# Last group of tiles exchanged and finished tile by tile, its stores halved over two queues; the weight preparation and the first loads rearranged

## The reference

```python
w = weights[conditions]                       # 64 rows of a table of 200, each 64 x 64
y = einsum('bct,bcd->bdt', x, w)              # x is 64 x 64 x 512 float32
a = quant_dequant_mxfp4(y.reshape(-1, 512))   # blocks of 32 along the last axis
w = quant_dequant_mxfp4(weight)               # 512 x 512
out = x + (einsum('mk,nk->mn', a, w) + bias).reshape(...)
```

## Time and profile before

| | |
|---|---|
| median of 3 runs | 98.33 us (97.95 to 99.38) |
| the profiled execution | 97.9 us |
| its span | 96.2 us (1.7 us lie around it) |
| busy: PE, DVE, ACT, POOL | 84.4, 81.9, 75.3, 32.9 us |
| chain that ended last, shares by engine | PE 44%, ACT 11%, DVE 10%, issue 6% |
| read from and written to HBM | 10.49 MB, 8.39 MB |

### The profile page before, as it was taken

One profiled execution on the slowest core, in us unless ns is written; L12 is line 12 of the kernel. 1 busy time (PEld: TensorE's weight loads), 2 busy tenths in 40 slices (PEclk: granted clock), 3 DMA queues, 4 the chain that ended last, 5 costly groups with the idle time before them and its releaser, 6 DMA issues.

```text
span 96.2 us, 2263 instructions
## 1 busy us (share of the span) xinstructions
PE 84.4 (88%) x715; PEld 41.2 (43%) x715; DVE 81.9 (85%) x138; ACT 75.3 (78%) x85; POOL 32.9 (34%) x60
## 2 busy tenths in 40 slices
PE   5999594999799998999899899989999989989800
PEld 4966252595482324344233433333352333445300
DVE  1248999999999999999999999999979999885600
ACT  4740498699998869999999999999999849957000
POOL 4273758399647548303000300320040021054000
PEclk9999999999999999999999999999999999999995
DMA  1898789694896789799999991896579399486992
GB/s 34 288 316 295 244 249 301 212 352 125 181 317 218 274 248 269 242 312 265 254 310 298 311 212 49 272 245 116 218 185 224 114 263 222 88 272 175 270 285 92
DMA packets 13901, 22.17 MB, mean 230 GB/s; under 512 B 4034, under 2 KB 4802, under 8 KB 13890
## 3 DMA queue, kind: packets, MB, share of 16 engines
q1 hardware_dynamic: 11456, 17.31, 56.4%
q0 software_dynamic: 2432, 4.73, 23.6%
q10 hardware_dynamic: 2, 0.00, 0.0%
HBM read 10.49 MB, written 8.39 MB: 196 GB/s over the span
## 4 chain that ended last, share of the span: by engine, by line
PE 44%; ACT 11%; DVE 10%; issue 6%; ACTq 0%; DVEq 0%
PE o_ps L357 20%; PE y_ps L357 5%; PE y_ps L306 5%; ACT y_sb L471 5%; ACT o_sb L493 4%; PE o_ps L352 4%; PE o_ps L337 3%; DVE a L654 3%; DVE n_int L625 2%; DVE top L645 2%; ACT z L463 1%; PE o_ps L382 1%; PE y_ps L367 1%; PE y_ps L300 1%; PE y_ps L318 1%
## 5 line engine op out<-in xcount | busy, mean ns | idle before, releaser
L357 PE MATMUL o_ps<-wT,aT 128*128 128x512 bf16 x100 | 23.8, 380 | 0.4 <-ACT aT L508 0.4
L183 POOL DMA_DIRECT2D mix<-in_L_cond_weights_dram x32 | 17.9, 560 | 12.4 <-issue 11.0
L625 DVE TENSOR_TENSOR n_int<-y_sb,inv 128x1024 int16<-128x1024 f32 (+1 forms) x17 | 19.5, 1155 | 0.2
L306 PE MATMUL y_ps<-x_sb,mix 64*64 64x512 f32 x120 | 15.6, 606 | 3.9 <-DMA mix<-in_L_cond_weights_dram 2.4
L272 POOL DMA_DIRECT2D x_sb<-o_sb x6 | 6.1, 1014 | 35.1 <-ACT o_sb L493 35.1
L382 PE MATMUL o_ps<-idle 128*128 128x128 bf16 x214 | 16.6, 235 | 1.2 <-DVE idle L664 1.2
L463 ACT ACTIVATE z<-y_ps 128x1024 bf16<-128x1024 bf16 x16 | 16.2, 1039 | 1.5 <-PE y_ps L306 1.2
L471 ACT COPY y_sb<-y_ps 128x1024 f32<-128x1024 f32 x16 | 16.3, 1035 | 0.0
L382 PEld LDWEIGHTS o_ps<-idle 128*128 128x128 bf16 x214 | 13.6, 105 | 5.1 <-issue 4.7
L480 ACT ACTIVATE zone<-inv 128x1024 int16<-128x1024 int16 (+2 forms) x11 | 11.6, 1074 | 3.8 <-DVE inv L618 3.8
L502 ACT COPY aT<-o_ps 128x1024 bf16<-128x1024 bf16 x14 | 13.7, 1045 | 1.0 <-PE o_ps L337 1.0
(11 more groups left out here) (52 smaller groups left out, 76.0 us busy)
## 6 DMA issues: line engine op xcount, KB each, us to landing
x_sb<-in_x_dram SPq DMA_DIRECT2D x7, 1024.0 KB, 6.4
out_dram<-x_sb SPq DMA_DIRECT2D x15, 256.0 KB, 3.6
x_sb<-o_sb POOLq DMA_DIRECT2D x6, 512.0 KB, 5.2
out_dram<-x_sb SPq DMA_DIRECT2D x6, 512.0 KB, 3.1
w_sb<-in_L_ffn_weight_dram SPq DMA_DIRECT2D x4, 256.0 KB, 3.4
x_sb<-in_x_dram SPq DMA_DIRECT2D x2, 512.0 KB, 6.6
out_dram<-x_sb POOLq DMA_DIRECT2D x4, 256.0 KB, 3.6
mix<-in_L_cond_weights_dram POOLq DMA_DIRECT2D x32, 16.0 KB, 4.5
```

The lines of the kernel that those rows point to most:

```text
L183: queue.dma_start(mix[HALVES[i % 2], first + i // 2, :], table[bass.ds(row, 1), :, :].rearrange("o c d -> (o c) d")).then_inc(mix_in[step] ...
L306: last = nc.tensor.matmul(y_ps[HALVES[g], 2 * q + r, :], mix[HALVES[r], (step - 1) * GROUP + n, :], x_tiles(step, n)[HALVES[r], :], start= ...
L357: last = nc.tensor.matmul(o_bank(step, t), aT[:, t, c, :], wT[:, c, :], start=False, stop=(c == KC - 1))
L625: nc.vector.tensor_tensor(columns(n_int, t, n), columns(y_sb[:, step % 2, :, :], t, n), columns(inv, t, n), ALU.mult).then_inc(n_done, 1)
```

## The change

The last step's second pair is exchanged like all others, so its residual and stores need x in exchanged order: a new tile `last_x` (1 MB) holds step 8's x once more, loaded by four DMAs behind all other loads on SP. DVE adds into it tile by tile, and each tile is stored in two DMAs of 64 partitions, one by SP and one by ACT; the last tile as two column halves, each again by both. In step 8 every stage is done tile by tile (before: first two together).

Step 7 is done in pairs: `limit` and `rescale` by pairs, transposes of a pair follow them, the products by pairs. Its first pair has the residual through PE and POOL stores it, as before. Of the second, tile 2 goes to `o_sb` and through an accumulating DMA (256 KB) and tile 3 is added by DVE and stored by SP. The store of step 6's second pair moves from SP to POOL.

At the start, `top_zone`, `invert`, `limit` and `zone` of W are done by pairs, the transposes of W's first pair move ahead of the second mixing, and the two loads of step 1's x move from SP to ACT, behind ACT's work on W's first two tiles. SP issues the mixing matrices of step 2 ahead of x of step 2. The range assertions are left out of `load_mixes`.

```diff
+        last_x = sb("last_x", [P, GROUP, T], F32)
...
             _, rows = nc.values_load_multi_w_load_instructions(
-                cond_sb[:, 2 * first:2 * (first + len(tiles))], engines=[engine], min_val=0, max_val=S - 1)
+                cond_sb[:, 2 * first:2 * (first + len(tiles))], engines=[engine], min_val=0, max_val=S - 1,
+                skip_runtime_bounds_check_because="cond holds row numbers of the table")
...
+        def store_last(queue, t, g, part, done):
+
+            queue.dma_start(exchanged_dram[LAST - 1, t // 2, g, t % 2, :, part], last_x[HALVES[g], t, part]
+                            ).then_inc(done, 16)
...
-            for h in range(2):
-                sp.dma_start(x_tiles(1, 2 * h, 2).rearrange("p (n t) -> p n t", n=2),
-                             x_dram[:, 2 * h:2 * h + 2, :]).then_inc(x_first_in[h], 16)
             sp.wait_ge(cond_in, 16)
             load_mixes(sp, mybir.EngineType.SP, sp_mix_in, 1, SP_TILES)
+            load_mixes(sp, mybir.EngineType.SP, sp_mix_in, 2, SP_TILES)
             load_x(2)
-            load_mixes(sp, mybir.EngineType.SP, sp_mix_in, 2, SP_TILES)
...
+            for q in range(2):
+                for g in range(2):
+                    sp.dma_start(last_x[HALVES[g], 2 * q:2 * q + 2, :],
+                                 exchanged_x_dram[LAST - 1, q, g, :, :, :].rearrange("r c t -> c r t")
+                                 ).then_inc(last_x_in, 16)
...
-                sp.wait_ge(x_added[step % 2], 16 * ((step + 1) // 2))
-                store(step, SUMMED, GROUP - SUMMED)
+                if step < LAST - 2:
+                    sp.wait_ge(x_added[step % 2], 16 * ((step + 1) // 2))
+                    store(step, SUMMED, GROUP - SUMMED)
+            sp.wait_ge(added, 1)
+            store(LAST - 1, GROUP - 1)
             for t in range(GROUP - 1):
-                sp.wait_ge(added, t + 1)
-                store(LAST, t)
+                sp.wait_ge(added, t + 2)
+                store_last(sp, t, 0, slice(0, N), stored)
             for half in range(2):
-                sp.wait_ge(added, GROUP + half)
...
+                sp.wait_ge(added, GROUP + 1 + half)
+                store_last(sp, GROUP - 1, 0, n_half(half), stored)
...
-            for q in range(2):
-                pool.wait_ge(late_copied, 2 * q + 2)
-                for g in range(2):
-                    pool.dma_start(exchanged_dram[LAST - 2, q, g, :, :, :].rearrange("r c t -> c r t"),
...
+            pool.wait_ge(late_copied, 2)
+            for g in range(2):
+                pool.dma_start(exchanged_dram[LAST - 2, 0, g, :, :, :].rearrange("r c t -> c r t"),
...
+            pool.wait_ge(late_tile, 1)
+            pool.dma_start(x_tiles(LAST - 1, SUMMED), o_sb[:, (LAST - 1) % 2, 0, :], accum_op=ALU.add
+                           ).then_inc(x_added[(LAST - 1) % 2], 16)
+            pool.wait_ge(x_added[(LAST - 2) % 2], 16 * ((LAST - 1) // 2))
+            n0 = (LAST - 3) * GROUP + SUMMED
+            pool.dma_start(out_dram[:, n0:n0 + 2, :], x_tiles(LAST - 2, SUMMED, 2).rearrange("p (n t) -> p n t", n=2)
+                           ).then_inc(late_stored, 16)
+            pool.wait_ge(x_added[(LAST - 1) % 2], 16 * (LAST // 2))
+            n0 = (LAST - 2) * GROUP + SUMMED
+            pool.dma_start(out_dram[:, n0, :], x_tiles(LAST - 1, SUMMED)).then_inc(late_stored, 16)
...
-            for t in range(GROUP):
+
+            for t in range(2):
                 z_w(t)
...
+                act.dma_start(x_tiles(1, 2 * t, 2).rearrange("p (n t) -> p n t", n=2),
+                              x_dram[:, 2 * t:2 * t + 2, :]).then_inc(x_first_in[t], 16)
+            for t in range(2, GROUP):
+                z_w(t)
+            zone_pair(1, 0)
+            z_pair(1, 0)
+            zone_pair(2, 0, 2)
+            z_pair(1, 1)
```

More of the change, by code:

```diff
@@ L149, in tiles_done, with after, late_part @@
             return GROUP * (step - 1) + t + 1
+        def after(step):
+            return step + 2
+        def late_part(part):
+            return after(LAST - 1) + part
         def n_half(half):
@@ L295, in mix_pair @@
                     pe.wait_ge(y_copied, tiles_done(step - 1, 2 * q + 1))
[L296 to L303, removed]
                 for i, (r, g) in enumerate(QUARTERS):
@@ L459, in z_pair @@
                 if q == 0 and step > 1:
-                    act.wait_ge(z_used, step - 1)
+                    act.wait_ge(z_used, after(step - 2))
                 act.wait_ge(y_ready, tiles_done(step, 2 * q + 1))
@@ L695, in _ @@
             lowest_zone(3)
[L696 removed]
+            lift(1, 3)
             top_zone(3)
[L698 to L701 removed]
+            invert(3)
+            for step in range(1, LAST - 1):
+                if step == 1:
+                    round_y(step, 0)
+                else:
                     tree_1(step + 1)
[L703 to L704 removed]
+                    round_y(step, 0)
                     tree_2(step + 4)
                 round_y(step, 2)
[L707 to L709 removed]
                 if step == 1:
+                    other_zones(step)
                     tree_1(step + 1)
[L712 removed]
+                    limit(step, after(step))
                     tree_2(step + 4)
[L714 removed]
+                    rescale(step, after(step), 2 * step + 2)
                     tree_3(step + 4)
@@ L718, in _ @@
                 else:
+                    tree_3(step + 4)
+                    other_zones(step)
                     block_max(step + 3)
-                    limit(step, step + 1)
+                    limit(step, after(step))
                     lowest_zone(step + 3)
-                    rescale(step, step + 1, 2 * step + 2)
-                lift(step + 1, step + 3).then_inc(z_used, 1)
+                    rescale(step, after(step), 2 * step + 2)
+                lift(step + 1, step + 3)
                 top_zone(step + 3)
-                invert(step + 2)
@@ new lines, in _ @@
+            other_zones(LAST - 1)
+            tree_2(LAST + 3)
+            limit(LAST - 1, after(LAST - 1), 0, 2)
+            tree_3(LAST + 3)
+            rescale(LAST - 1, late_part(0), 2 * LAST, 0, 2)
+            block_max(LAST + 2)
+            limit(LAST - 1, after(LAST - 1), 2, 2)
+            lowest_zone(LAST + 2)
+            rescale(LAST - 1, late_part(1), 2 * LAST, 2, 2)
+            lift(LAST, LAST + 2)
+            top_zone(LAST + 2)
+            invert(LAST + 2)
+            round_y(LAST, 0, 1)
@@ new lines, in _ @@
+            limit(LAST, after(LAST), 0, 1)
+            for t in range(1, GROUP):
+                round_y(LAST, t, 1)
+                rescale(LAST, late_part(1 + t), 2 * LAST + t, t - 1, 1)
+                limit(LAST, after(LAST) + t, t, 1)
+            rescale(LAST, late_part(1 + GROUP), 2 * LAST + GROUP, GROUP - 1, 1)
+            dve.wait_ge(o_ready, tiles_done(LAST - 1, GROUP - 1))
+            nc.vector.tensor_tensor(x_tiles(LAST - 1, GROUP - 1), o_bank(LAST - 1, GROUP - 1),
+                                    x_tiles(LAST - 1, GROUP - 1), ALU.add).then_inc(added, 1)
```

284 lines of the change are left out of this document (143 added, 141 removed).

## The result

The changed kernel takes 99.7 us (median of 4 runs, 99.28 to 99.8), the one before 98.14 us: a ratio of 1.017, 95% interval 1.011 to 1.022. The forecast was 97.5, and 99.7 lies above its range. Two more sets of runs of the same changed kernel gave 99.68 us (ratio 1.024, interval 1.003 to 1.045) and 100.18 us (1.021, 1.015 to 1.027). It is slower, by 1.6 to 2.4 us. Some executions of these programs are in a slower state: medians here are of all runs, ratios and their intervals leave the slower ones out. The profiled execution has a span of 97.8 us, where it was 96.2.

A forecast was written before the change was run, and what follows sets the result against it. No engine alone was taken as the bound; the end was as much DMA work as last sum. From the profiled 97.9 us, start -0.35 and end by DMA -0.05 gave 97.5, range 95.6 to 98.9.

The forecast's parts named there:

- The start: W's work by pairs before step 1 fills DVE's and ACT's waits: 0.85 to -0.2 us gained, 0.35 taken.
- Rival 3: Start gains nothing because W's last tiles wait for x, up to 0.2 us worse: 98.05 us, chance 0.19.
- The end, computing path: Steps 7 and 8: work by pairs and tiles removes waits; last sum at 89.6 instead of 91.45, 1.8 us earlier.
- The end, DMA work: Last stores: 10.66 us of DMA work instead of 7.4 keeps the end late, gaining only 0.05 us.
- End of data: Last stores: data from 84.6 us plus 10.66 us of DMA work end at 95.25, set at 95.3.
- rival 4: POOL's last store in step 7 waits for a late accumulation: at worst 99.7 to 100.0 us, chance 0.06.
- The halves over two queues: Last stores in halves from SP and ACT: same bytes, only issue time saved, taken as no gain; left open.
- Rival 2: DMA keeps up and the last sum sets the end, 4.8 us following it: 95.75 us, chance 0.25.

The follow-up runs named there:

- head_on_before: Kernel before with only the change's start edits (all edits before step 1's products): 99.25 us, ratio 1.001.
- t2_zone: tile2_dve with ACT's zones of W's second pair ahead of step 1's z, and DVE's last a of W ahead of step 1's maxima: 96.35 us, 0.981.
- t2_accum: tile2_dve plus one 256 KB accumulating DMA by POOL between idle tiles, waited for only at the end: 98.53 us, repeated 98.54 us.
- tile2_dve: Changed kernel with step 7's tile 2 summed by DVE and stored by SP with tile 3, without POOL's accumulation and last store: 97.17 us, 0.985.
- after_b: The changed kernel itself, run again on one chip beside the last set of experiments: 100.18 us, ratio 1.021.
- acc_sp_store_b: Changed kernel with step 7's accumulated tile 2 stored by SP behind its other stores instead of by POOL, repeated in the last set: 98.61 us, 1.003.
- pool6_on_before: Kernel before with only the store of step 6's second pair moved to POOL, between its stores of step 7's pairs: 99.54 us, 1.012.
- t2_sp6: tile2_dve with the store of step 6's second pair given back to SP: 97.46 us, ratio 0.992.
- sp_store6: Changed kernel with the store of step 6's second pair given back to SP: 100.19 us, ratio 1.014.
- one_queue: Changed kernel with all ten stores of the last group issued by SP, none by ACT: 99.73 us, ratio 1.0095.
- t2_zone_hw: t2_zone without any DMA of POOL's after step 6's accumulation: 96.50 us, ratio 0.985.
- t2_hw: t2_sp6 with step 7's first pair stored by SP too, so POOL issues no DMA after step 6's accumulation: 98.15 us.

## Why the prediction was wrong

**The start: -0.35 forecast, no gain seen.** Step 1's transposes are at 26.22 in the changed kernel and 26.50 in head_on_before, against 26.09. The DVE distances were right up to the second `inv` (11.7 against 11.9). What failed is the half sentence "with ACT's half `zone` and `z` of step 1 between": I let ACT be ready for the zones. PE's mixing of a pair is done 1.2 us after it starts (11.27 to ACT's `z` at 12.50), so ACT's in-order queue holds the zones until 13.42. t2_zone shows it: the two exchanges bring the transposes to 25.52, 0.6 before the 26.09 of the kernel before, where my upper end was 0.85. Rival 3's reason was wrong: W's last tiles did not come late (DVE took them at 7.36), though its size was right. Leaving out the assertions and issuing earlier gave no time that head_on_before can show.

**The end, computing path: the time was right, in part by luck.** Forecast last sum 89.6 before any gain of the start, measured 89.39 with none. But PE began step 7's transposes at 76.76, not 77.3, since it was done with step 6 earlier, and the residual that I took for 0.54 us held PE from 77.30 to 78.32, 1.0 us. The two errors of half a microsecond cancel in the 79.09 at which the products start.

**The end, DMA work: the sum was right (10.66 against 10.5 us), two steps from it to the time were not.** The forecast puts the end of the span at 95.8 us; it was 97.77.

The first step is "End of data: 84.6 + 10.66 = 95.25", as if every engine were full until the last byte. POOL's first store was issued at 83.14, so the data began no later than assumed, yet the engines were at 0.74 from 92 to 96 us and the last byte of SP's and ACT's stores moved at 96.5: these stores come late into the queues. Single issues took up to 2.6 us instead of 0.5 to 0.6, the last began 3.6 us after the last sum, and it landed 4.0 us later, at 96.97. I said of issue time that it "does not matter where data queue up"; here the last issue was late although its data were ready.

The second step is in rival 4: "At the medians the landing is 93.5, and it hides." That path sets the end. The accumulation landed after 5.0 us, near the median of 5.2, but POOL's store behind it landed after 5.7 us, not 3.6, at 95.44. Then comes a term that the forecast puts at nothing: POOL's DRAIN, which ended 2.1 us after that landing. Even at the forecast's medians, 93.5 + 2.1 and 0.2 for the barrier make 95.8, level with the forecast end and not hidden. The kernel before had it too: its DRAIN on POOL ended at 95.99, SP was done at 95.94.

What the runs separate: the accumulation of one tile costs 1.4 to 2 us (t2_accum against tile2_dve, forecast 1.37). POOL's late store costs 1.6 us more than the same store by SP (after_b against acc_sp_store_b) where the price difference is 0.36; this term was mis-sized by four. Their two traces divide it. In after_b POOL's DRAIN ended at 98.18, 0.85 us after SP was done at 97.33; in acc_sp_store_b it ended at 94.38, and SP was last at 96.15. That is half of it. The other half, 0.8 us, lies in SP's and ACT's own stores: from the last sum to the time when SP is done it is 7.3 us in after_b and 6.5 in acc_sp_store_b. That POOL's packets hold up the issues of the other two queues is what the rows suggest (L204's rows last 5.9 us in acc_sp_store_b, 6.8 in after_b); no run shows it by itself. Step 6's store by POOL costs 1.2% in pool6_on_before, but nothing in tile2_dve against t2_sp6, and nothing that can be told in sp_store6. Why it costs in one kernel and not in the others stays open.

**The halves over two queues.** I let the rule of the Trainium skill (DMA: Bandwidth & Descriptors, "Issuing engines are not separate DMA queues") stand for 0, and in the changed kernel one_queue agrees that the second queue brings nothing. In tile2_dve the same edit costs 1.9 to 3.5 us. The rule of the Trainium skill allows for it, for it says that a second engine saves issue time; its word that this is usually small does not hold for ten issues of 0.6 us behind the last sums.

**Rivals.** Rival 2 (the last sum sets the end) is what tile2_dve is: 97.2 with no gain of the start. Rival 4 named the right path and also the number, 99.7, but the number is luck: it took 7.4 and 5.4 us for the two landings at worst, they took 5.0 and 5.7, and the 2.1 us of POOL's DRAIN made up for it.

## What to carry to other kernels

Behind the last sum, count DMA work as engine time and take the slower kinds (an accumulation, a store from POOL) out of the last microseconds first: 256 KB accumulated and stored by POOL cost 2.5 us or more here, and one sum of 0.7 us on DVE with a store by SP replaced both. Follow each engine that issues DMAs to its own end: POOL was done only 2.1 us after its last store had landed. Then look at the issues: with 10.5 us of DMA work at the end, the issue of the last store was late though its data were long ready, and with 8.5 us of it, ten issues of 0.6 us on one queue were the bound and a second queue was worth 1.9 to 3.5 us. And in an order written by hand, an operation that is moved earlier on one engine needs the same move on the engine that feeds it.

## What was not expected of the hardware

In all 18 traces of this case the DRAIN with which POOL closes the program ended 1.9 to 2.1 us after the landing of its last DMA, whether that landed at 83.5 us (t2_zone_hw) or at 97.0 (sp_store6); SP's took 7 ns.

A DMA issue from SP or ACT that takes 0.5 to 0.6 us at its shortest took up to 2.3 and 2.6 us with POOL's packets in the queues; in t2_hw, with none of them, still up to 1.1 and 1.4. In 84 to 96 us POOL's 1.57 MB, 256 KB of it accumulated, took 52.0% of the engines' time and 1.30 MB of SP's and ACT's 35.5%, so 3.97 against 3.28 us per MB. And the time from last sum to end of span is 4.8 to 5.1 us in the traces of the kernel before, tile2_dve, t2_hw, t2_zone and t2_zone_hw, with 8.5 and 8.2 us of DMA work in the second and third, so some 5 us may be the floor of that tail with these stores; no run shows what sets it.
